# A convolution with weights made per pixel: logits stored tap by tap, an element-wise running maximum, a tenth tap for GpSimd, and two chunks at once in the first window

## The reference, cut to what matters

```python
sub2 = x1[:, :, None] - unfold_patches(x2)          # 32 channels, 49 taps
subp = p[:, :, None] - unfold_patches(p)            # 2 position channels
feat = jnp.concatenate([sub2, subp], axis=1)
y = relu(bn_eval(feat, ...)); y = conv1x1(y, cw1)   # 34 -> 32
y = relu(bn_eval(y, ...)); wgt = softmax(conv1x1(y, cw2, cb2), axis=2)   # over 49 taps
for i in range(7):
    for j in range(7):
        out = out + patch(x3p, i, j) * wgt[:, :, idx][:, :, None]
```

## Time and profile before

| | |
|---|---|
| median of 3 runs | 3922.48 us (3919.37 to 3923.53) |
| the profiled execution, its own time and its span | 3920.62 us, span 3918.8 us |
| first matmul of `conv_stage`, last product into `osb` | 193.4 us, 1771.4 us |
| from one `fold` to the next | 106.8 us, 13 times |

### The profile page before, as it was taken

How to read it: one execution, slowest core, us unless ns; L and a number is a source line. 1 busy time by engine, 2 the same in 40 slices (tenths; PEclk the granted TensorE clock), 3 DMA queues, 4 the chain that set the end, 5 groups by cost and what they waited for, 6 DMA issues and landing times. The chain is left out here.

```text
span 3918.8 us, 101868 instructions
## 1 busy us (share of the span) xinstructions
PE 3247.8 (83%) x42750; PEld 1559.7 (40%) x42750; DVE 2532.1 (65%) x2271; ACT 2038.2 (52%) x3476; POOL 1827.0 (47%) x948
## 2 busy tenths in 40 slices
PE   4649888888888898865899899989998999379897
PEld 1214343344444443432433343334433342256675
DVE  6218888888888889895645664566556553554411
ACT  1146666655555666632575556556655666352320
POOL 1137888888888888871422042103301240234332
PEclk9859999999999999997999999999999999689998
DMA  5610111111111111102111111110112010335443
GB/s 200 193 47 24 59 58 56 56 52 56 55 49 57 51 40 59 49 12 92 26 26 53 48 26 26 62 55 10 26 62 63 1 26 24 117 127 180 139 150 116
DMA packets 169631, 257.40 MB, mean 66 GB/s; under 512 B 81780, under 2 KB 128796, under 8 KB 166124
## 3 DMA queue, kind: packets, MB, share of 16 engines
q1 hardware_dynamic: 157120, 219.82, 18.6%
q0 software_dynamic: 11392, 31.02, 2.5%
q10 hardware_dynamic: 684, 0.05, 0.0%
HBM read 152.29 MB, written 79.27 MB: 59 GB/s over the span
## 5 line engine op out<-in xcount | busy, mean ns | idle before, releaser
L654 DVE TENSOR_TENSOR prod<-ps,win 128x3584 f32<-128x3584 f32 x280 | 1085.7, 3887 | 180.2 <-PE ps L711 110.6
L711 PE MATMUL ps<-prod,ident 32*32 32x504 f32 x17920 | 1038.7, 630 | 144.9 <-issue 70.1
L997 POOL TENSOR_TENSOR phk<-kv 128x768 f32<-128x768 f32 (+1 forms) x200 | 347.6, 1740 | 1090.7 <-ACT kv L1086 999.3
L711 PEld LDWEIGHTS ps<-prod,ident 32*32 32x32 f32 x17920 | 413.0, 107 | 404.6 <-issue 344.7
L1128 ACT ACTIVATE phq<-ps 128x896 f32<-128x896 f32 x448 | 384.2, 917 | 199.9 <-PE ps L1394 199.1
L463 POOL TENSOR_TENSOR ex<-lg,mx 128x1568 f32<-128x1568 f32 x98 | 426.0, 4373 | 28.0 <-DVE mx L640 27.8
L453 POOL TENSOR_TENSOR y<-a1w,x2w 128x1568 f32<-128x1568 f32 x98 | 320.0, 3275 | 181.0 <-PE ps L694 163.6
L689 PE MATMUL ps<-y,cw1bd 32*32 32x392 f32 x3136 | 332.6, 836 | 59.3 <-DMA cwp<-cw1p 34.0
L578 ACT ACTIVATE y<-ps,u2c,s2c 128x784 f32<-128x784 f32 x196 | 196.8, 1004 | 269.9 <-PE ps L694 269.9
L1394 PE MATMUL ps<-qst,sel 96*128 96x448 bf16 x1120 | 291.9, 364 | 25.9 <-ACT phq L1128 7.2
L480 POOL TENSOR_TENSOR own_a<-ex,win 128x1792 f32<-128x1792 f32 x70 | 259.8, 3711 | 104.5 <-PE ps L711 71.2
(11 more groups left out here) (253 smaller groups left out, 5062.1 us busy)
## 6 DMA issues: line engine op xcount, KB each, us to landing
win<-planes SPq DMA_DIRECT2D x14, 2480.0 KB, 8.8
pf<-pf_dram SPq DMA_DIRECT2D x392, 55.1 KB
qst<-qsp SPq DMA_DIRECT2D x96, 196.0 KB, 4.6
planes<-stage SPq DMA_DIRECT2D x7, 1984.0 KB, 7.2
xs<-in_x SPq DMA_DIRECT2D x8, 1568.0 KB, 21.3
conv_dram<-osb SPq DMA_DIRECT2D x56, 224.0 KB
t<-in_x SPq DMA_DIRECT2D x28, 448.0 KB, 3.9
xn<-conv_dram SPq DMA_DIRECT2D x28, 448.0 KB, 6.2
```

The costliest lines, as they stand in the source:

```text
L654: v.tensor_tensor(o, w, xw, ALU.mult).then_inc(prod_ready, 1)
L711: mm = pe.matmul(ps[32 * h:32 * h + 32, 4 + r, 0:DENC], diag(ident, r), x[32 * r:32 * r + 32, h].rearrange("p s w -> p (s w)"), start=begi ...
L997: pool.tensor_tensor(phk[j % 2][0:r, :, ROT_V * DH:FLIN].rearrange("p h (r i) -> p h r i", i=DH), ki.unsqueeze(2).broadcast_to([r, HPG, RO ...
```

## The change

Six edits, all but the first in `conv_stage`.

1. The position features are made tap by tap, so `ud` is a plain subtraction.
2. `lg` and `run` lie tap by tap (row of the window, tap, pixel). PE's `first` reads `y` and writes PSUM without the rearrangement; POOL's `shift` reads `lg` in the order in which it lies.
3. The maximum is taken element-wise: no instruction for row 0, then `run = max(lg[1], lg[0])` and `run = max(lg[i], run)` for i = 2 to 6, each over 1568 elements with both inputs in SBUF. `fold` is a tree over the 7 taps: 4 x 168, 4 x 112 and 224 elements, three instructions, each waiting for the one before.
4. `OWN` is 10: GpSimd multiplies ten taps, and DVE 39. DVE still has 20 pair instructions in a window, the last with one tap. PE takes the own taps at u = 10 to 19 (before 11 to 19). The last own tap is now written to `osb`.
5. In the first slot, where there is no b, chunks alternate between banks 0, 1 and 4, 5 and between `y2` and a part of `prod`. PE and ACT run a loop of their own there.
6. The three constant matrices are loaded by one DMA each instead of four (7 DMAs on ACT's queue, before 16).

```diff
-OWN = 9
+OWN = 10
...
-        lg = sb("lg", [P, K7, PW, K7])
+        lg = sb("lg", [P, K7, RW, K7, W])
...
-                pool.tensor_tensor(ex[:, i], l, m, ALU.subtract).then_inc(shifted, 1)
+                pool.tensor_tensor(ex[:, i], lg[:, i], m, ALU.subtract).then_inc(shifted, 1)
...
-                    v.tensor_reduce(run[:, :, i], lg[:, i], AX.X, ALU.max).then_inc(ranmax, 1)
+                    if i > 1:
+                        v.wait_ge(ranmax, NMAX * a.n + i - 1)
+                    v.tensor_tensor(run[:], lg[:, i], lg[:, 0] if i == 1 else run[:], ALU.max).then_inc(ranmax, 1)
...
-                    v.wait_ge(ranmax, K7 * (a.n + 1))
+                    v.wait_ge(ranmax, NMAX * a.n + K7 - 1)
+                    v.tensor_tensor(run[:, :, 0:3], run[:, :, 0:3], run[:, :, 4:7], ALU.max).then_inc(ranmax, 1)
+                    v.wait_ge(ranmax, NMAX * a.n + K7)
+                    v.tensor_tensor(run[:, :, 0:2], run[:, :, 0:2], run[:, :, 2:4], ALU.max).then_inc(ranmax, 1)
+                    v.wait_ge(ranmax, NMAX * a.n + K7 + 1)
                     if b:
                         v.wait_ge(shifted, K7 * a.n)
-                    v.tensor_reduce(mx[:], run[:], AX.X, ALU.max).then_inc(maxed, 1)
+                    v.tensor_tensor(mx[:].rearrange("p (h w) -> p h w", w=W), run[:, :, 0], run[:, :, 1], ALU.max).then_inc(maxed, 1)
...
-                            pe.matmul(ps[at:at + 32, r // 2, 0:CW].rearrange("p (w j) -> p w j", j=K7), diag(cw1, r),
-                                      y[32 * r:32 * r + 32, :, h * W:(h + 1) * W].rearrange("p j w -> p w j"), start=True, stop=False)
+                            pe.matmul(ps[at:at + 32, k + r // 2, 0:CW].rearrange("p (j w) -> p j w", w=W), diag(cw1, r),
+                                      y[32 * r:32 * r + 32, :, h * W:(h + 1) * W], start=True, stop=False)
...
+                if b is None:
+                    first(0)
+                    first(1)
+                    for c in range(NCH):
+                        second(c)
+                        if c + 2 < NCH:
+                            first(c + 2)
...
-                act.dma_start(cw1[q, :], cw1_bd[q, q]).then_inc(w_in, 16)
-                act.dma_start(cw2[q, :], cw2_bd[q, q]).then_inc(w_in, 16)
-                act.dma_start(ident[q, :], ident_dram[q, q]).then_inc(w_in, 16)
```

More of the change, by code:

```diff
@@ L223, in _ @@
             v.wait_ge(pstep, 3)
[L224 to L225 removed]
+            v.tensor_tensor(ud[:], pq[:, 0, :], pq[:, 1, :], ALU.subtract).then_inc(pstep, 1)
             v.tensor_scalar(vd[:], hq[:, 1:1 + K7], hq[:, 0:1], -1.0, ALU.subtract, ALU.mult).then_inc(pstep, 1)
@@ L341 @@
 SCALE_AT = 1
+NMAX = K7 + 1
 class Blk:
@@ L430, in diag, with chain_bank @@
             return t[32 * r:32 * r + 32, :]
+        def chain_bank(b, c):
+            return 4 * (c % 2) if b is None else 0
         def slots(eng, slot):
@@ L573, in second @@
                 def second(c):
-                    g = a.g(c)
+                    g, k = a.g(c), chain_bank(b, c)
                     act.wait_ge(mm1, g + 1)
-                    if not (a.early(1) and c < 1):
+                    if b is None:
+                        if c >= 2:
+                            act.wait_ge(mm2, g - 1)
+                    else:
                         act.wait_ge(mm2, g)
-                    act.activation(y2[:], ps[:, 0:2, 0:CW], ACT.Relu, scale=s2c[:], bias=u2c[:]).then_inc(relu2, 1)
+                    o = y2_odd if k else y2[:]
+                    act.activation(o, ps[:, k:k + 2, 0:CW], ACT.Relu, scale=s2c[:], bias=u2c[:]).then_inc(relu2, 1)
                 def third(c):
                     act.wait_ge(mm2, a.g(c) + 1)
-                    i, h = c // 2, c % 2 * 2
+                    i, h, k = c // 2, c % 2 * 2, chain_bank(b, c)
                     if b and c % 2 == 0:
                         act.wait_ge(shifted, b.q(i) + 1)
-                    act.activation(lg[:, i, h * W:(h + 2) * W].rearrange("p (h w) j -> p h (w j)", w=W), ps[:, 0:2, 0:CW],
+                    act.activation(lg[:, i, h:h + 2].rearrange("p h j w -> p h (j w)"), ps[:, k:k + 2, 0:CW],
                                    ACT.Identity, bias=par[:, CB2:CB2 + 1]).then_inc(logit, 1)
-                for u in range(NPAIR_D):
+                if b is None:
+                    first(0)
+                    for c in range(NCH):
+                        second(c)
+                        if c >= 1:
+                            third(c - 1)
+                        if c % 2 == 0 and c + 2 < NCH:
+                            first(c // 2 + 1)
+                    third(NCH - 1)
+                    expo(a, 0)
+                    expo(a, 1)
+                for u in range(NPAIR_D if b else 0):
                     if a and u in CH_AT:
@@ L682, in first @@
                         pe.wait_ge(pf_in[a.qpar(i)], 16 * B * a.qhalf(i))
-                    if not (a.early(1) and c < 1):
+                    k = chain_bank(b, c)
+                    if b is None:
+                        if c >= 2:
+                            await_ge(logit, a.g(c) - 1)
+                    else:
                         await_ge(logit, a.g(c))
@@ L699, in second @@
                     await_ge(relu2, a.g(c) + 1)
+                    m = chain_bank(b, c)
+                    y = y2_odd if m else y2[:]
                     for k in range(2):
@@ L702, in second @@
                             at = 64 * k + 32 * (r % 2)
-                            mm = pe.matmul(ps[at:at + 32, r // 2, 0:CW], diag(cw2, r), y2[32 * r:32 * r + 32, k, :], start=True, stop=True)
+                            mm = pe.matmul(ps[at:at + 32, m + r // 2, 0:CW], diag(cw2, r), y[32 * r:32 * r + 32, k, :], start=True, stop=True)
                     mm.then_inc(mm2, 1)
```

18 lines of the change are left out of this document (11 added, 7 removed).

## The result

| | before | after |
|---|---|---|
| median | 3923.01 us (3919.37 to 3924.28, 4 runs) | 3866.80 us (3861.22 to 3871.84, 4 runs) |
| first matmul of `conv_stage` | 193.43 us | 185.71 us |
| first and last `mx` | 277.7, 1666.1 us | 234.0, 1614.1 us |
| `mx` to `mx` | 106.8 us | 106.2 us |

The ratio is 0.9861 (95% interval 0.9846 to 0.9876): 56 us less, where 70 were forecast. The profiled execution's span is 3859.4 us (before 3918.8). The total comes near; the parts do not. The first slot gave 43.7 us with the earlier start (forecast 23), and the thirteen slots with two windows gave 8.3 together (forecast 45). The conv stage ends 57.5 us earlier: its last product into `osb` ends at 1713.9, not 1771.4. `mx` is timed here by the start of its last instruction, which lasts 0.39 us after the change and 1.79 before; by its end, the first slot gave 1.4 us more and the last one 1.4 less.

The account below looks back on a forecast made before the run. Two stretches bound the slot: the chunk chain through PE and ACT, and the end chain from POOL's shifts to PE's next product. Savings 7 (DMAs) + 16 (first slot) + 45 (thirteen slots) + 2 (last slot) = 70 us: 3852, range 3768 to 3893.

Parts of the forecast that it names:

- The maximum at u = 11: Two-window slots: this DVE maximum meets a POOL own tap just begun and waits it out, 3.7 us.
- about 12 us of waiting, of which 6.3 reach the period: 103.3: Two-window slots: DVE and POOL taking turns over SBUF lengthen the slot from 97.0 to 103.3 us.
- 97.0: Two-window slot without contention: 106.8 us less 7.6 for PE's reading in order and 2.2 for two shifts.
- four of six maxima for unhindered: Two-window slots: four of DVE's six maxima find POOL idle or nearly done, because POOL waits for PE there.
- `first` on the lower clock stays at about 1.9: First slot: with PE's 2.8 this makes 4.7 us a chunk against 5.9, 13 times, saving 16 us.
- 3.3 a chunk and 34 us: First slot if PE's clock rises: ACT becomes the bound at about 3.3 us a chunk, 34 us saved.
- I count no gain from reading in order: First slot at the lower clock: PE's in-order read gives nothing, since L689 and L703 both take 1.56 for sixteen.
- A: Rival, two-window slots: DVE and POOL don't hinder each other, or only POOL is stretched; 3770 us, or 3795; chance 0.30.
- C: Rival, two-window slots: POOL goes first every time, slot 111 us, kernel slower at 3956 us; chance 0.08.
- D: Rival, PE's `first`: the matmul doesn't gain from reading in order; slot about 105 us, kernel 3878 us; chance 0.10.
- E: Rival, whole kernel: no change, because 11.7 us of DVE and POOL waiting reach the slot's period; chance 0.05.
- B: The forecast itself: DVE and POOL take turns over SBUF, slot 103.3 us, kernel 3852 us; chance 0.47.

Follow-up runs that it names:

- flat_max: Changed kernel with one-input maximum reductions over seven neighbouring pixels of one tap, not the true maxima; 3849.84 us against 4004.07 before, ratio 0.9620.
- first_slot: Kernel before with only the first slot's two chunks in flight and the seven DMAs; 3883.53 us against 3922.65, ratio 0.9897.
- busy_pe: Kernel before with extra PE matmuls, their results unread, filling PE's waits in the first slot; 3900.47 us in one run.
- act_turns_nine: Changed kernel with ACT storing logits pixel by pixel, the maxima of before and nine own taps; 3884.28 us against 3924.92 before, ratio 0.9900.
- pe_in_order: Kernel before with only PE's `first` reading `y` in order, taps and pixels then mixed up; 3824.66 us in one run.
- pe_turns: first_slot with PE's `first` reading in order and writing PSUM in a stride of 7 elements; 3864.67 us against 4005.94 before, ratio 0.9651.
- flat_nine: flat_max with nine own taps instead of ten; 3762.53 us against 3924.92 before, ratio 0.9585.

## Why the prediction was right and wrong

*The mechanism of the forecast was right.* DVE and POOL take turns, and `mx` is ready 85.6 us after PE's first product in the slot shown (887.04 to 972.60), where 87 was forecast; without the turns, in flat_max, it is 76.9 (941.12 to 1018.01), forecast 76. The maximum at u = 11 waits out an own tap, as forecast; the one at u = 13, forecast to wait for half of one, finds POOL idle. What the forecast cites from the Trainium skill's "SBUF — State Buffer", section "Who interferes with whom", one lock for a two-input DVE instruction and a GpSimd one, held for a whole instruction, agrees with the 5.19 and the 1.93 us above; flat_max shows the page's other half, that a DVE reduction with one input does not hinder POOL.

*Its size in the slots was wrong: 8.3 us in all, not 45.* The step that failed is "about 12 us of waiting, of which 6.3 reach the period: 103.3". Two terms of the sum were too small. Without contention the mean slot is 98.2 and not 97.0. With it, 8.0 us reach the period, not 6.3. 1.2 + 1.7 = 2.9 us, thirteen times, are about the 37. In the slots shown: the own taps ahead of the shifts end 82.4 us after PE's first product in flat_max, not 81, and 89.4 in the change (887.04 to 976.4), not 87; the tail from there to the next first product is 17.2 in flat_max and 16.8 in the change, where the forecast's 97.0 and 103.3 leave 16.0 and 16.3. The slot of 106.2 lies outside the forecast's own two us either way of 103.3. By lengths, the DVE instructions for the maximum are stretched by 5 x 0.98 + 1.05 + 3.36 = 9.3 us a slot, and nearly all of it counts: from 908.23 to `mx` DVE is idle for 0.5 us only. The forecast took four of six maxima for unhindered; in the slot shown the one at u = 7 takes 2.95 and those at u = 15 and 17 2.58 each, beside a shift or an own tap begun 2.3 to 2.8 us before, and only two, at u = 9 and 13, are unhindered.

*The first slot was undersized: 36 us, not 16.* The failed step is "`first` on the lower clock stays at about 1.9". The text had the other case, 3.3 a chunk and 34 us, if the clock rises; it did, and a chunk takes 3.1. The cause is shown by first_slot, where a chunk takes 3.8 and the clock rises, and by busy_pe, where the clock rises and 11 us are gained with one chunk in flight. act_turns_nine shows that the rise is not certain with two. "I count no gain from reading in order" fell with it: 8.0 us, because the stride's cost stays when the clock rises; at 0.50 it holds, with 0.7 us in pe_in_order.

*Right:* PE's first matmul (186 forecast, 185.71), so the seven DMAs; the matmul near 500 ns and steps near the forecast 4.3 us while PE is the bound (4.3 to 4.5: 895.16, 899.45, 903.84, 908.29 in the changed kernel); the tenth own tap, at nothing that the noise lets see, in three pairs of kernels; no gain from five of the seven shifts, by pe_turns and flat_nine. The shift came to 3.55 instead of 3.28 us, 0.5 a slot on the end chain. The last slot gave 5.5 instead of 2: 1.4 of it is the way `mx` is timed, the rest no run takes apart.

*The rivals.* A is refuted as a description of the changed kernel, but its price was good: flat_max, which takes the contention away, stands at 0.962, that is 3774 us on a chip where before takes 3923, against A's 3770; that too hides two errors, a slot of 98.2 for 97.0 and a first slot that gave more. C (POOL always first) is refuted: the turns alternate. D is refuted by 505 ns. E's 11.7 us of waiting would make a slot of 97.0 + 11.7 = 108.7; 106.2 lies between B and E, and would by itself, with the forecast's first slot, have given 70 - 37 = 33 us. The total lies nearer to B only through the first slot.

So the total came out well partly by luck: two errors, -37 and +20, offset each other. What remains open is how the 8.0 us of the period divide between the steps; only replacing the tree, 1.8, was measured apart.

## What to carry to other kernels

When a rearrangement makes one engine pay, try it at every place of the chain before changing the layout for all: here the same turn cost PE 0.33 us a matmul on the read, ACT 0.8 on the store, DVE 1.4 on the read, POOL 0.8 on the read, and PE nothing on the write. An element-wise maximum over two SBUF tensors is not the equal of a reduction of the same length if GpSimd is busy beside it: compare them with the second engine running, and look for the wait inside the lengths, not in the idle time. And where PE works in short bursts at a granted clock of 0.50, a second chunk in flight can bring more than the waits it removes; price both cases, give the risen clock its due chance, and look whether it stays: in act_turns_nine it fell back.

## What the runs showed of the hardware

- PE reading a moving operand in a stride of 224 elements of 4 bytes: 835 ns for 392 columns against 505; sixteen of them 1.56 and 1.54 us at granted clocks of 0.50 and 1.00, where those read in order go from 1.56 to 0.89. Writing PSUM in a stride of 7 elements: 507 ns, no cost.
- ACT storing 784 elements to SBUF in a stride of 7: 1708 ns against 914.
- DVE's reduction of 1568 elements: 1777 ns over neighbours, 3169 in a stride of 56 elements.
- POOL's `ex<-lg,mx`: 4375 ns with `lg` in a stride of 7, 3549 in order. The second stays above `z`'s 3273 with no DVE instruction in its way; that the broadcast `mx` causes this is a guess that no run tested.
- Maxima of 1568 elements on DVE with two inputs in SBUF: 1.78 us with POOL idle, 5.19 when issued 0.17 us behind a POOL tap of 3.72.
- A copy of 224 elements on POOL: 0.38 us, and up to 1.95 behind a two-input DVE maximum.
